# Cross attention with a routed FFN on one core: pairs of heads one by one, maxima ahead of small work, weights loaded later

## The reference, cut to what matters

```python
def xattn(query, key, value):            # query = layernorm(x), key = value = ctx
    q, k, v = (proj_blocks(a, W) for ...)          # 16 heads of 16, blocks of 64 tokens
    scores = einsum('bhpqd,bhpkd->bhpqk', q[rows], k[cols]) * 16 ** -0.5
    attn = softmax(scores)                         # for each pair of blocks by itself
    ob = einsum('bhpqk,bhpkd->bhpqd', attn, v[cols])
    return segment_sum(ob, rows) @ Wo.T            # sum over the blocks that a row block sees

x = x + xattn(layernorm(x), ctx, ctx)
y = layernorm(x)
top1 = argmax(y @ gate_w.T)                        # two experts
routed = relu(y @ w1[top1] + b1[top1]) @ w2[top1] + b2[top1]
shared = relu(y @ sw1 + sb1) @ sw2 + sb2
out = x + routed + shared
```

## Time and profile before

| what | us |
|---|---|
| median of 3 runs | 938.26 |
| their lowest and highest | 934.51, 942.17 |
| the profiled execution | 933.05 |
| its span, first to last instruction | 931.1 |
| mean granted clock of TensorE | 0.944 of full |

### The profile page before, as it was taken

One profiled execution on the slowest core, in us unless ns is written; L12 is line 12 of the kernel. 1 busy time (PEld: TensorE's weight loads), 2 busy tenths in 40 slices (PEclk: granted clock), 3 DMA queues, 4 the chain that ended last, 5 costly groups with the idle time before them and its releaser, 6 DMA issues.

```text
span 931.1 us, 24363 instructions
## 1 busy us (share of the span) xinstructions
PE 797.0 (86%) x8374; PEld 680.0 (73%) x8374; DVE 600.2 (64%) x1242; ACT 486.1 (52%) x1124; POOL 422.9 (45%) x773
## 2 busy tenths in 40 slices
PE   3366877789898999999999989899999999989894
PEld 3345666577877878786868787787878687868794
DVE  5656467676858586867777675858586776745331
ACT  3363534537465555556464646555464647365452
POOL 5543423424446263737364453627373544455311
PEclk8586989999999999999999999999999999999998
DMA  8666231344536353444444453534433544414630
GB/s 282 168 173 235 80 103 48 99 139 133 164 115 193 96 154 124 138 157 122 148 147 134 141 164 113 192 92 147 134 117 132 157 137 139 144 47 148 224 106 23
DMA packets 97387, 128.19 MB, mean 138 GB/s; under 512 B 14655, under 2 KB 82623, under 8 KB 97088
## 3 DMA queue, kind: packets, MB, share of 16 engines
q1 hardware_dynamic: 89760, 107.89, 37.7%
q0 software_dynamic: 6624, 18.95, 6.2%
q10 hardware_dynamic: 960, 0.79, 0.4%
HBM read 90.80 MB, written 37.04 MB: 137 GB/s over the span
## 4 chain that ended last, share of the span: by engine, by line
PE 55%; DVE 18%; DMA 12%; issue 6%; ACT 4%; POOL 2%; SPq 1%; DVEq 1%; ACTq 1%; POOLq 0%
PE acc L724 15%; PE hid L535 12%; PE nd L638 9%; PE work L535 5%; DVE nmax L1178 5%; DVE T L1197 4%; DMA scratch_q<-T 4%; PE work L622 3%; DVE T L1194 3%; PE work L666 2%; PE work L544 2%; PE work L591 1%; PE nd L591 1%; DMA QP<-scratch_m 1%; PE work L652 1%
## 5 line engine op out<-in xcount | busy, mean ns | idle before, releaser
L1456 POOL TENSOR_TENSOR hl<-h,hh 128x256 fp32r<-128x256 f32 x228 | 166.0, 733 | 328.4 <-ACT hh L981 328.0
L1197 DVE RECIPROCAL T<-nd 128x256 f32<-128x256 f32 x64 | 112.3, 1755 | 55.9 <-PE nd L638 50.9
L981 ACT ACTIVATE h<-hid,bias 128x256 f32<-128x256 f32 x144 | 69.0, 479 | 103.7 <-PE hid L535 103.7
L535 PE MATMUL hid<-Xs,W 128*128 128x256 f32 x816 | 113.7, 295 | 1.1
L724 PE MATMUL acc<-w_hi,hh 128*128 128x256 f32 (+1 forms) x528 | 114.1, 298 | 0.0
L965 ACT ACTIVATE PT<-work 128x512 f32<-128x512 f32 x192 | 99.8, 593 | 24.1 <-PE work L622 22.6
L1178 DVE TENSOR_REDUCE nmax<-work 128x8 f32<-128x512 f32 x128 | 82.2, 684 | 45.1 <-PE work L591 44.8
L535 PEld LDWEIGHTS hid<-Xs,W 128*128 128x128 f32 x816 | 107.7, 203 | 4.1 <-issue 3.1
L724 PE MATMUL acc<-w_lo,hh 128*128 128x256 f32 (+1 forms) x528 | 106.6, 284 | 0.0
L535 PE MATMUL hid<-Xr,W 128*128 128x256 f32 x768 | 104.4, 285 | 0.0
L535 PEld LDWEIGHTS hid<-Xr,W 128*128 128x128 f32 x768 | 94.2, 188 | 4.7 <-DVE Xr L1131 0.2
(11 more groups left out here) (191 smaller groups left out, 1620.1 us busy)
## 6 DMA issues: line engine op xcount, KB each, us to landing
W<-w1q SPq DMA_DIRECT2D x64, 512.0 KB, 6.1
KP<-scratch_k SPq DMA_DIRECT2D x192, 64.0 KB, 2.5
QP<-scratch_q SPq DMA_DIRECT2D x180, 64.0 KB, 2.3
scratch_k<-T SPq DMA_DIRECT2D x16, 512.0 KB, 3.5
scratch_q<-T SPq DMA_DIRECT2D x16, 512.0 KB, 3.2
yt<-yq SPq DMA_DIRECT2D x17, 260.0 KB, 2.8
xt<-xq SPq DMA_DIRECT2D x17, 256.0 KB, 3.8
xin<-x SPq DMA_DIRECT2D x16, 256.0 KB, 3.5
```

The costliest lines, as they stand in the source:

```text
L535: mm = nc.tensor.matmul(dst, R(s), R(m), start=n == 0, stop=n == len(steps) - 1)
L981: last = nc.scalar.activation(dst, hid[:, u % 2, a, :], ACT.Relu, bias=bias[:, 2 * u + a:2 * u + a + 1])
L1197: nc.vector.reciprocal(T[:, p, :], nd[:, p % 2, 1, :]).then_inc(sem["inverted"], 1)
L1456: nc.gpsimd.tensor_tensor(R(hl[:, u % 2, a]), h32[:, u % 2, a], hh[:, u % 2, a], ALU.subtract).then_inc(sem["hl_done"], 1)
```

## The change

- Attention: `scores_t(0)`, then for each pair p: scores of p+1, in every second pair a `fill`, values of p. ACT's exponentials run one pair ahead in the same way. Pair 6 goes to GUESSED for i >= 3.
- In the iterations with a tile, visit 0 of the next element stands before `tile_up` 3.
- DVE's `gate_scores` 1, `move_ids`, `choose` and `finish_tile` go from the end of an iteration to behind the maxima of the next visit 1, `norm1_apply` behind those of visit 2, `rank_tokens` behind maximum 13; PE's `ranks` stand before visit 3.
- `table_relu` is made before the last guess.
- Weights: five stages (`h32` twice, `yp`, `yt`, `xt`) throughout, loads from the first q bounce on; constants behind the spread of k; ACT's and DVE's first splits later; POOL's last two pieces behind `reciprocal_deviation`; ACT's wait for two low parts ahead of the first exponentials is gone.
- Tile after the last iteration: tokens are loaded behind W1 and the bias.

```diff
-GUESSED_EARLY, GUESSED = (1, 3, 5, 7), (1, 3, 5, 7)
+GUESSED_EARLY, GUESSED = (1, 3, 5, 7), (1, 3, 5, 6, 7)
...
-STAGES, LATE_STAGES = 7, 3
-SLOTS = [n % STAGES for n in range(2 * STAGES)]
-SLOTS += [n % LATE_STAGES for n in range(W1_PIECES + W2_PIECES - len(SLOTS))]
+STAGES, BY_VECTOR = 5, 14
+SLOTS = [n % STAGES for n in range(W1_PIECES + W2_PIECES)]
...  SP, load_tile
-                    if u == 0:
+                    if u == 0 and not at:
                         sp.wait_ge(sem["x_queued"], 32 * (m + 1))
                         load_tile_x(m, row)
...
                 sp.dma_start(bsel[:, :], b1[:, bass.ds(HT * expert + HT, HT)]).then_inc(sem["bias_loaded"], 16)
+                if at:
+                    sp.wait_ge(sem["x_queued"], 32 * (m + 1))
+                    load_tile_x(m, row)
...  PE
-                    ranks(n, claim(i, ("rk", 0), tile=tile))
                 visit(i, 2, more)
                 if shared:
                     shared_down(n, 0)
                     shared_up(n, 2)
+                    ranks(n, claim(i, ("rk", 0), tile=tile))
                 visit(i, 3, more)
...
-                for group in range(GROUPS):
-                    scores_t(i, 2 * group, more)
-                    scores_t(i, 2 * group + 1, more)
-                    if more or group > 1:
-                        fill(n, m, tile, group, expert)
-                    values(i, 2 * group)
-                    values(i, 2 * group + 1)
+                scores_t(i, 0, more)
+                for p in range(PAIRS):
+                    if not tile and p % 2:
+                        fill(n, m, tile, (p + 1) // 2, expert)
+                    if p + 1 < PAIRS:
+                        scores_t(i, p + 1, more)
+                    if tile and p % 2 == 0 and (more or p > 2):
+                        fill(n, m, tile, p // 2, expert)
+                    values(i, p)
...
                 attention_out(i, more)
+                if more:
+                    visit(i + 1, 0)
                 if tile:
                     tile_up(m, 3)
-                if more:
-                    visit(i + 1, 0)
...  ACT
-                for group in range(GROUPS):
-                    for j in range(4):
-                        exps(i, 4 * group + j)
-                    if tile and more and group < 2:
-                        tile_relu(m, group)
-                    guess_inverse(i, 2 * group + 1)
-                    if shared and not tile and group == 3:
+                exps(i, 0)
+                exps(i, 1)
+                for p in range(PAIRS):
+                    if p + 1 < PAIRS:
+                        exps(i, 2 * p + 2)
+                        exps(i, 2 * p + 3)
+                    if tile and more and p in (0, 2):
+                        tile_relu(m, p // 2)
+                    if p in guessed(i):
+                        guess_inverse(i, p)
+                    if shared and not tile and p == 6:
                         table_relu(i - 1)
...  DVE
                     for j in range(4 * v, 4 * v + 4):
                         maximum(i, j)
+                        if shared and j == 13:
+                            rank_tokens(n)
                     splits(i, v + 1)
+                    if v == 1 and (type(i) is not int or i > 3):
+                        finish_tile(m - 1)
                     if shared and v == 1:
-                        rank_tokens(n)
+                        gate_scores(n, 1)
+                        if type(i) is not int or i > 1:
+                            move_ids(n - 1)
+                        choose(n)
+                    if shared and more and v == 2:
+                        norm1_apply(i + 1)
...
                 shared_low(i)
-                gate_scores(i, 1)
-                if shared:
+                if not more:
+                    gate_scores(i, 1)
                     move_ids(n)
-                choose(i)
-                if tile and more:
-                    finish_tile(m)
+                    choose(i)
...
-                if norm1:
-                    norm1_apply(i + 2)
...  POOL
-                for k in range(3 if shared else 5, 11):
+                for k in range(3 if shared else 5, 10):
                     splits(i, k)
...
                 reciprocal_deviation(i, 1)
+                splits(i, 10)
...
-            pool.wait_ge(sem["zeroed"], 3)
-            for n in range(LATE_STAGES + 2):
-                load(n)
...
-            for n in range(LATE_STAGES + 2, STAGES):
+            reciprocal_deviation(1, 0)
+            pool.wait_ge(sem["first_q_bounced"], 16)
+            for n in range(STAGES):
                 load(n)
-            reciprocal_deviation(1, 0)
```

More of the change, by code:

```diff
@@ L219, in stage @@
         def stage(n, like):
-            s = (h32[:, 0], h32[:, 1], yp[:, :, :], *(PT[:, k] for k in range(4)))[SLOTS[n]]
+            s = (h32[:, 0], h32[:, 1], yp[:, :, :], yt[:, :, :], xt[:, :, :])[SLOTS[n]]
             return flat(s)[:, 0:512].rearrange("p (a b) -> p a b", a=2)
@@ L228, in by_vector @@
         def by_vector(n):
-            return n % 2 == 1 and n < 2 * STAGES
+            return n % 2 == 1 and n < BY_VECTOR
         def low_done(n):
@@ L450, in _ @@
             sp.dma_start(x1[:, 0, :], indicator).then_inc(sem["indicator_loaded"], 16)
[L451 to L457, removed]
             load_x(1)
@@ L465, in _ @@
                 spread_k(half)
+            sp.wait_ge(sem["proj_lo"], 4)
+            for dst, src in ((bias1[:, :], b1), (bsum[:, :], blocksum), (hsum[:, :, :], headsum),
+                             (gate[:, :, :], bass.AP(tensor=gate_w.tensor, offset=0, ap=[[0, P], [D, 2], [1, D]])),
+                             (x1[:, 1, :], bass.AP(tensor=b2.tensor, offset=0, ap=[[0, P], [1, D]])),
+                             (flat(mT), bass.AP(tensor=b2.tensor, offset=D, ap=[[0, P], [1, D]])),
+                             (bias2[:, :], bass.AP(tensor=b2.tensor, offset=2 * D, ap=[[0, P], [1, D]])),
+                             (ids[:, :], places[:, 0:TT]), (PT[:, 0, 0, 0:P], places[:, TT:TT + P])):
+                sp.dma_start(dst, src).then_inc(sem["consts_loaded"], 16)
             sp.wait_ge(sem["consts_read"], 1)
@@ L603, in maxima @@
             def maxima(i):
+                if type(i) is int and i == 0:
+                    pe.wait_ge(sem["consts_read"], 1)
                 bank = claim(i, ("mT", 0))
@@ L1091, in _ @@
             projection_high(3)
-            for n in range(EARLY_PIECES):
-                split_high(n)
             act.wait_ge(sem["first_q_bounced"], 16)
@@ L1099, in _ @@
             front_v(0, acc[:, :, :])
+            for n in range(EARLY_PIECES):
+                split_high(n)
             iteration(0, False, False, True)
@@ L1383, in _ @@
             projection_low(3)
-            nc.vector.tensor_copy(before16[:, :], xt[:, 0, 0:P])
+            norm1_stats(1)
+            norm1_apply(1)
+            for j in range(4):
+                maximum(0, j)
+            dve.wait_ge(sem["consts_loaded"], 16 * 9)
+            nc.vector.tensor_copy(before16[:, :], PT[:, 0, 0, 0:P])
             nc.vector.tensor_tensor(bias2[:, :], bias2[:, :], x1[:, 1, :], ALU.add).then_inc(sem["bias_summed"], 1)
@@ L1392, in _ @@
                     split_low(n)
-            norm1_apply(1)
-            for j in range(4):
-                maximum(0, j)
             splits(0, 1)
```

14 lines of the change are left out of this document (3 added, 11 removed).

## The result

The changed kernel takes 923.87 us (median of four runs, 923.02 to 924.62), the kernel before took 937.53 beside it (median of four, 934.51 to 942.17). The ratio is 0.988, with an interval of 0.984 to 0.992: faster by 1.2%. The forecast was 917, so the time lies in the range and in the likeliest case's own range. But two of its five steps (A and B) came out with the wrong sign, and C and D, put at 2 together, gave 12.

The account below looks back on a forecast made before the run. A steady iteration was taken as PE's own work plus its waits for DVE, with falls to the lower clock. From 933.05, -5 -8 +0 -2 -3 = -18 gives 915, with 2 for the median 917; range 891 to 936.

Parts of the forecast that it names:

- the likeliest case: The forecast itself for the whole kernel: 917 us, its own range 906 to 928, chance 0.48.
- A: Start: PE's wait of 6.29 becomes 2.40 and q's spread shrinks, while DVE waits for constants; sum -5, bounds -10 to +6.
- B: Tables of iterations 1 and 2: early `table_relu` removes most of the 2.94 wait, twice; -4 each, -8 in sum.
- C: Attention pairs one by one, iterations 3 to 15: +0.5 ahead of `attention_out`, half covered; 0 per iteration, bounds -1.0 to +2.0.
- D: DVE's small work behind the maxima, eleven steady iterations: +1 from waits, -3 from fewer falls of the clock; -2.
- rival 3: Start: weights come too late and hold up iteration 0, +6 in place of -5; 928 us, chance 0.12.
- 1 may come back: Tables: POOL's 2.37 behind the table is hidden only in part by the first sixteen products, so 1 may return.
- the 2 for the clock: Tables, interval 2: of 4.9 lost at the lower clock, 2 counted as regained, within the -4 each.
- missed meeting at 1.05: Before the second half of `attention_out`: if DVE's L1194 and POOL's low parts miss each other, 1.05 goes; not counted.
- I count four of eleven in place of six: Steady iterations: the lower clock still comes behind the wait around visit 3, but in four intervals, not six; -3.
- E: Behind the last iteration: the bias is issued earlier, PE's 4.22 falls to one or two; -3, bounds -2 to -5.
- The 2 added for the median: Whole kernel: the runs' median lay 5.2 above the profiled execution; 2 of that added to the sum of 915.

Follow-up runs that it names:

- run 6: Changed kernel with the nine constants loaded ahead of the first bounce, the residual behind the spread's first half, the bias first at the end: 921.49 us, ratio 0.985.
- run 1: Changed kernel with DVE's moved small work, `rank_tokens` and PE's `ranks` back where they stood before: 927.06 us, ratio 0.990.
- run 4: Changed kernel with pairs in groups of two again and the old order of loads for the tile after the last iteration: 939.08 us, ratio 1.004.
- run 5: Changed kernel with `gate_scores` 1 ahead of the maxima, early constants, residual behind the spread's first half, and pairs in twos again: 909.24 us, ratio 0.971.

## Why the prediction came out as it did

**A, start: wrong, the term was "DVE then waits for constants that are issued only behind the spread ... I count 1 for it".** DVE's, SP's and PE's timelines of after:

```profile
35.07 0.23 DVE L1401 CAST before<-PT 128x128 bf16<-128x128 f32 x1 [4.91 <-DMA PT<-places]
```
```profile
27.32 0.43 SPq L468 DMA_DIRECT2D PT<-places  x1
```
```profile
40.72 0.80 PE L594 MATMUL work<-KP,QP 48*128 48x256 f32 x4 [6.85 <-DVE nmax L1186]
```

The last of nine loads is issued at 27.32 and lands 7.73 later, beside the weights. DVE waits 4.91 for it between the first maxima. The price is about 5.8, the difference between the mean first transposes of the variants with late and early constants (50.1 and 44.3); run 6 alone shows 5.6. The rest of A held in part: with early constants, run 6 has its first transposes and interval 1 at 99.30 in all, 1.8 less than before (96.4 to 101.2 in the seven variants), and PE's wait of 6.29 is 3.46 after the change. The sum moved as in rival 3: PE's transposes of xhat, set at "after 87", start at 91.62. But it was not the weights that were late, for run 6 loads them as the changed kernel does.

**B, tables: wrong, the step was "-4 each".** The wait itself went as forecast, from 2.94 to 0.84, ended by POOL as "1 may come back" had it. PE's timeline shows what took its place in interval 2, and DVE's what it does shortly before the end:

```profile
129.41 0.64 PE L643 MATMUL nd<-PT,V 128*32 128x256 f32 x8 [0.62 <-DVE T L1207]
...
135.16 1.20 PE L781 MATMUL acc<-w_hi,hl 128*128 128x256 f32 x8 [0.84 <-POOL hl L1474]
...
139.18 0.50 PE L594 MATMUL work<-KP,QP 48*128 48x256 f32 x4 [1.79 <-DMA QP<-scratch_q]
...
145.35 0.46 PE L547 MATMUL work<-id,xhat 128*128 128x128 f32 x2 [2.39 <-issue]
...
160.46 0.30 PE L611 MATMUL work<-id,nmax 128*128 128x128 f32 x1 [1.93 <-DVE nmax L1186]
```
```profile
156.45 1.28 DVE L1159 TENSOR_SCALAR xhat<-xin,mv,rstd 128x256 f32<-128x256 f32 x2
```

Values now wait for DVE's divisions (0.40, 0.62, 0.72), where before they waited 1.35 for exponentials. The spread of q, which SP issues behind a residual that waits for DVE, ends 1.79 late; run 6 shows that this hangs on the residual. The wait of 2.39 for the tokens stayed, and the clock falls behind it in both intervals. In interval 2 it fell behind the table before, and the mean clock rose from 0.91 to 0.94; in interval 3 it is 0.94 as before. So the 2 for the clock came at most once. The text also reckoned the small work of D for the steady iterations alone. Here `norm1_apply` stands between the last maxima as well, and PE waits 1.93 and 0.39 before L611, where it waited 0.75 and nothing; in run 1, with the small work back, these two are 0.37 and nothing. How much is due to each is not settled: equal code gave up to 3 us of difference in these two intervals.

**C, pairs: 0 forecast, and the parts right.** The stretch from scores to `attention_out` grew by 0.7 (forecast 0.5). The wait was said to stay "mostly"; it fell from 1.46 to 0.59, since DVE's last instruction is held up by one of POOL's instructions and not by both (0.74 in place of 1.48). That turns on little: in most intervals it begins 0.27 behind POOL, where before it mostly began 0.21 to 0.23 behind. Net -0.3 per undisturbed interval (49.74 before, 49.45 in run 1). The text put a missed meeting at 1.05 and did not take it.

**D, small work: the mechanism right, the clock mis-sized.** The forecast was that each small instruction waits for one of POOL's, that PE then waits 1.3 to 2.0 before and in visit 3, and that a net 0.1 is lost. Measured: 1.4 of hold-up for the two halves of `gate_scores`, `move_ids` and `choose`, where the text had 1.3 to 2.0, and 0.4 or 1.0 for `norm1_apply`, which its sum left out; waits of 0.6 to 0.7 at visit 3 and up to 0.7 before L611; net +0.07. The Trainium skill, SBUF — State Buffer, Who interferes with whom, names such pairs of instructions, and the trace agrees with L1229 at 0.42 and 0.95. It also says that whichever issues first keeps the shared ports. By the starts in the trace that does not hold here: `norm1_apply` was held up although first by 0.05, and not when first by 0.12, and in run 4 L1195 was held up although first by 0.15. The failed term is "I count four of eleven in place of six": none falls. It was taken over from the sum of the waits (1.3 for 1.23), and their place and grouping changed as well. The one long wait that might have kept the falls alive, at `attention_out`, is one that C shortened, and the text did not join the two.

**E, end: -3 forecast, -2.7 between the means** of kernels with either order, although the two profiles show 1.1. In place of PE's 4.22 behind the bias stand these two on its timeline of after:

```profile
869.16 1.11 PE L547 MATMUL work<-id,xt 128*128 128x128 f32 x4 [2.75 <-DMA xt<-xq]
...
877.16 0.50 PE L769 MATMUL acc<-level,level_row 128*128 x2 [1.50 <-DVE yp L1265]
```

The tokens end last, as said; their scatter takes 7.09 beside the four quarters of W1 and took 4.81 before.

So the time lies in the range by luck, because errors cancelled: A and B together came out 18 worse than forecast, C and D 10 better. The profiles moved by 8.3 where the sum had 18, the medians by 13.7. The 2 added for the median measured -0.75, for the profiled execution of the changed kernel lies above its median. All runs of before spread over 928.8 to 942.4, the four of the changed kernel over 1.6 us, which agrees with falls of the clock as the cause of the spread, but does not show it.

## What to carry to other kernels

When constants move behind other loads, ask who reads them first and what is queued behind the reader: nine loads of 1 to 256 KB cost 5.8 us here. Small DVE work with its operands in SBUF has a price that depends on what POOL does at that moment; move it into POOL's idle time, one instruction at a time, and look at its duration in the new place. Here the clock fell in five or six of eleven intervals as long as either of two waits was left (runs 1, 4 and 5), so judge two edits that each shorten a wait together.

## What the runs showed of the hardware

A fall of the granted clock from 2.4 to 1.2 GHz followed one wait of 1.55 to 1.74 us in some intervals of run 5, and two of 0.5 and 0.7 with half a visit's products between them in some of the kernel before and of run 1. Behind waits of 0.6 to 0.7 some 4 us apart none followed in the steady intervals, and none behind the waits of 1.46 to 1.66 at `attention_out` in the kernel before, which has `tile_up` 3 behind that wait and not visit 0. So the length of a wait does not decide by itself; what does, and why a fall comes in some iterations and not in all, the runs do not show. A fall costs 1.6 to 1.7 per interval. The hold-up of `norm1_apply` by POOL is decided within a tenth of a microsecond (POOL 0.05 behind: 1.69, 0.12 behind: 1.14), so edits elsewhere, such as one guess more, move a steady iteration by 0.55. For L1195 the border lies elsewhere: with POOL 0.15 behind it still waited for both of POOL's instructions (1.85).
